# Fewer, longer loads at the head of a vision-tower kernel: chunks three and four of the embedding together, two late weights in whole rows

## The chip, the cores and the metric

One core of a Trainium2 chip runs the whole kernel in one launch. The metric is device time in microseconds (us); the host only lays the arrays out beforehand. Before the change three runs took 125.57, 114.17 and 115.2 us, a median of 115.2 us. The execution that the profiler recorded took 115.0 us, of which 112.8 us are the span of the trace.

## The reference

The input is 16 images of 3x96x96. One transformer block runs on them, with a norm after each half:

- **Embedding.** Each image becomes 36 patches of 768 numbers, times a 768x192 weight, plus a bias.
- **Windowed attention.** 12 heads of 64, a window of 65 tokens, an output weight of 768x192, a residual and a layer norm.
- **Mixture of three attention experts.** Each has 64 channels and a causal mask; the first has a convolution over its queries, the second global keys, the third a position bias (used for at most 64 tokens). A gate picks two of the three. A 192x192 projection, a residual and a layer norm end it.

```python
h = _L0_tok_ref(x, L0_tok_Wp, L0_tok_bp)
h = _layernorm(h + _L0_attn_ref(h, L0_attn_w_qkv, L0_attn_w_out, L0_attn_b_out), axis=-1)
h = _layernorm(h + _L0_ffn_ref(h, ...), axis=-1)
```

## The kernel before, in words

**Tiling.** The 16 images are two groups (g = 0, 1) of eight, 288 tokens each. The 768 patch features are six chunks (k = 0 to 5) of 128, one on each partition row. So `x_f[128, 2, 6, 288]` holds the input and `tw_f[128, 6, 256]` the embedding weight; the weight is 192 wide, and the host repeats its last 64 columns to make 256.

**Split numbers.** TensorE works on a high and a low part of each float32. ScalarE (ACT) makes the high part by a copy, then VectorE (DVE) or GpSimd (POOL) the low part by a subtraction. For embedding chunk n this is step `xs n` on both: ACT writes `tw_hi` (L462) and `x_hi` (L464), DVE `tw_lo` (L648) and `x_lo` (L651). `xs 0` to `xs 5` are the six chunks of group 0 and `xs 6` to `xs 11` those of group 1, whose weights are there already. Step `em n` on TensorE (L884) multiplies chunk n: two halves of the output by three products of high and low parts, six matmuls, each 288 columns wide. Ahead of them TensorE runs 20 warm-up matmuls (L868) and three that clear banks (L871, L873).

**Order.** Three tables, `PE_ORDER`, `ACT_ORDER` and `DVE_ORDER`, set by hand what each engine does after what; an engine that waits holds all that is behind it. They begin:

```python
em 0, em 1, em 2, em 3, em 4, em 5, em 6, em 7, qk 0, em 8, qk 1, em 9, s 0, s 1, v 0 0, qk 2, em 10   # PE
xs 0, xs 1, xs 2, xs 3, xs 4, xs 5, wq 0, xs 6, xs 7, xs 8, wq 1, hh 0, xs 9, cq 0, wv 0, xs 10, wq 2   # ACT
```

`qk` projects queries and keys, `wq` splits their weights, `hh` reads the embedded tokens out, `cq` copies queries and keys, `wv` splits the value weight (L472, then DVE L657 and L659), and `v 0 0` is the first matmul that needs it (L920).

**Loads.** The sync engine (SP) issues nearly every load, one after the other (L367 to L385); ACT issues the first two pieces of the embedding weight. The pieces of group 0's chunks are `X_PIECES`, and `SP_TOK` says which pieces of the weight SP issues. Each piece has a semaphore of its own, so the split of a chunk begins when its piece has landed. After them come biases, query and key weights for the first head pair, group 1's input in two pieces (`X_LATER`, chunks 0 to 2 first: L373) and further weights; the last large ones are `wo_f` (the attention's output weight, L381) and `ffn_f` (the experts' weights, L382), and behind these three small ones, `posb` among them, which DVE reads for `posmask` (L680). The output weight is laid out by the host as six rows of 256 numbers on a partition, the experts' as two rows of 1088; the kernel loads the first 192 and the first 1024 of each row. ACT splits them at L476 (`wo 0`) and L480 (`wf 0`), POOL at L444, L409 and L411.

Of the kernel before, what the change touches and what calls it, by code (L numbers as in the profile page):

```python
# [34 lines left out]
F32 = mybir.dt.float32  # L35
F32R = mybir.dt.float32r
BF16 = mybir.dt.bfloat16
ALU = mybir.AluOpType
ACT = mybir.ActivationFunctionType
# [5 lines left out]
DIM, NCH = 192, 2  # L45
DUP = 256
PATCH, PK = 768, 6
PAIRS, HD = 6, 64
# [14 lines left out]
F_PROJ = F_VAL + DIM  # L63
F_END = F_PROJ + DIM

X_PIECES = [slice(0, 1), slice(1, 2), slice(2, 3), slice(3, 4), slice(4, 6)]
X_LATER = [slice(0, 3), slice(3, 6)]
QK_PIECES = [slice(0, 1), slice(1, 2), slice(2, 4), slice(4, 6)]
WARM_UP = 20
ACT_TOK, SP_TOK = (0, 1), (2, 3, 4)  # L70
TILE_IMAGES = [(0, 3), (3, 6), (6, 8)]
TILES = len(TILE_IMAGES)
ROWS = 3 * TOK
# [71 lines left out]
def vit_tower(nc, x_t, tok_w, w_qk, w_v, w_out, f_w, f_g2, f_bv, pos_bias, biases, consts, bf_consts, out_t):  # L145
    with ExitStack() as ctx:
        def sb(name, shape, dt=F32):
            return ctx.enter_context(nc.sbuf_tensor(name, shape, dt))

        def sem(name):  # L150
            return ctx.enter_context(nc.semaphore(name))
# [12 lines left out]
        wv_f = sb("wv_f", [128, NCH, PATCH])  # L164
        wv_hi = sb("wv_hi", [128, NCH, PATCH], F32R)
        wv_lo = sb("wv_lo", [128, PATCH], F32R)
        wo_f = sb("wo_f", [128, PAIRS, DIM])
        wo_hi = sb("wo_hi", [128, PAIRS, DIM], F32R)
        wo_lo = sb("wo_lo", [128, PAIRS, DIM], F32R)
        ffn_f = sb("ffn_f", [128, NCH, F_END])  # L170
        ffn_hi = sb("ffn_hi", [128, NCH, F_END], F32R)
        ffn_lo = sb("ffn_lo", [128, F_END], F32R)
        fg2_w = sb("fg2_w", [33, 3])
# [63 lines left out]
        ld_const, ld_wv, ld_wo, ld_ffn, ld_small = (sem(s) for s in ("ld_const", "ld_wv", "ld_wo", "ld_ffn", "ld_small"))  # L237
        ld_x = [[sem(f"ld_x{g}{n}") for n in range(len(pieces))] for g, pieces in enumerate((X_PIECES, X_LATER))]
        ld_tok = [sem(f"ld_tok{n}") for n in range(len(X_PIECES))]
        ld_qk = [sem(f"ld_qk{n}") for n in range(len(QK_PIECES))]  # L240
# [4 lines left out]
        qk_hi, qk_lo, wv_hi_s, wv_lo_s, wo_hi_s, wo_lo_s = (  # L245
            sem(s) for s in ("qk_hi", "qk_lo", "wv_hi_s", "wv_lo_s", "wo_hi_s", "wo_lo_s"))
        posmask_s, image_s, conv_b_s = sem("posmask_s"), sem("image_s"), sem("conv_b_s")
        ffn_hi_s, ffn_lo_s, h1_hi_s, h1_lo_s = (sem(s) for s in ("ffn_hi_s", "ffn_lo_s", "h1_hi_s", "h1_lo_s"))
# [99 lines left out]
        def leaving(z):  # L348

            return slice(tile_cols(LEAVE_TILES[z][0]).start, tile_cols(LEAVE_TILES[z][-1]).stop)  # L350
# [8 lines left out]
        def piece_of(g, k):  # L359
            return [n for n, ks in enumerate((X_PIECES, X_LATER)[g]) if ks.start <= k < ks.stop][0]  # L360

# [3 lines left out]
        @block.sync  # L365
        def _(sp):
            for n, ks in enumerate(X_PIECES):  # L367
                if n in SP_TOK:
                    sp.dma_start(tw_f[:, ks], tok_w[:, ks]).then_inc(ld_tok[n], 16)
                sp.dma_start(x_f[:, 0, ks], x_t[:, 0, ks]).then_inc(ld_x[0][n], 16)  # L370
            sp.dma_start(bias[:], biases).then_inc(ld_bias, 16)
            sp.dma_start(wqk_f[:, QK_PIECES[0]], w_qk[:, QK_PIECES[0]]).then_inc(ld_qk[0], 16)
            sp.dma_start(x_f[:, 1, X_LATER[0]], x_t[:, 1, X_LATER[0]]).then_inc(ld_x[1][0], 16)  # L373
            sp.dma_start(wqk_f[:, QK_PIECES[1]], w_qk[:, QK_PIECES[1]]).then_inc(ld_qk[1], 16)
            sp.dma_start(x_f[:, 1, X_LATER[1]], x_t[:, 1, X_LATER[1]]).then_inc(ld_x[1][1], 16)
            sp.dma_start(bfc[:], bf_consts).then_inc(ld_const, 16)
            sp.dma_start(const[:, 0:C_MEAN], consts[:, 0:C_MEAN]).then_inc(ld_const, 16)
            sp.dma_start(wv_f[:], w_v).then_inc(ld_wv, 16)
            for n in (2, 3):
                sp.dma_start(wqk_f[:, QK_PIECES[n]], w_qk[:, QK_PIECES[n]]).then_inc(ld_qk[n], 16)  # L380
            sp.dma_start(wo_f[:], w_out[:, :, 0:DIM]).then_inc(ld_wo, 16)  # L381
            sp.dma_start(ffn_f[:], f_w[:, :, 0:F_END]).then_inc(ld_ffn, 16)  # L382
            sp.dma_start(fg2_w[:], f_g2).then_inc(ld_small, 16)
            sp.dma_start(bv_all[:], f_bv).then_inc(ld_small, 16)
            sp.dma_start(posb[:], pos_bias).then_inc(ld_small, 16)  # L385
            for g in range(GROUPS):
                for z, done in enumerate((outs_a, outs_d)):
                    part = leaving(z)
                    cols = slice(g * GT + part.start, g * GT + part.stop)
                    sp.wait_ge(done, NCH * g + 1)  # L390
                    sp.dma_start(out_t[0:128, cols], out_s[:, g, 0, part]).then_inc(st_out, 16)
                    if (g, z) != (GROUPS - 1, 1):
                        sp.wait_ge(done, NCH * g + 2)
                        sp.dma_start(out_t[128:DIM, cols], out_s[0:64, g, 1, part]).then_inc(st_out, 16)
            sp.wait_ge(st_out, 32 * GROUPS * len(LEAVE_TILES))

        @block.gpsimd
        def _(pool):
            pool.memset(g1_t[:], 0.0).then_inc(zeroed, 1)
            pool.memset(k_t[:, :, :, TOK:KEYS], 0.0).then_inc(zeroed, 1)  # L400
            pool.memset(edges[:], 0.0).then_inc(zeroed, 1)
            pool.memset(wgt_last[:], 0.0).then_inc(zeroed, 1)
            pool.wait_ge(zeroed, 4)
            pool.memset(g1_t[32:33], 1.0).then_inc(zeroed, 1)
            pool.wait_ge(zeroed, ZEROED)

            def lo_part(lo, hi, raw, done, before):

                nc.gpsimd.tensor_tensor(lo, raw[:, 0], hi[:, 0].bitcast(F32), ALU.subtract).then_inc(done, 1)  # L409
                pool.wait_ge(done, before + 1)  # L410
                nc.gpsimd.tensor_tensor(hi[64:128, 1], raw[64:128, 1], hi[64:128, 1].bitcast(F32),  # L411
                                        ALU.subtract).then_inc(done, 1)
                pool.wait_ge(done, before + 2)

            def pair_lo(p):
                pool.wait_ge(qk_hi, p + 1)
                lo_part(wqk_lo[:, p], wqk_hi[:, p], wqk_f[:, p], qk_lo, 2 * p)

            def residual_rows(g, lo_done, col):
                pool.wait_ge(lo_done, NCH * g + NCH)  # L420
                n = pool_sums[0]
                pool_sums[0] += 1
                for c in range(NCH):
                    nc.gpsimd.tensor_tensor(h_res[:, g, c], hcols(h_hi, g, c).bitcast(F32),  # L424
                                            bias[:, col + c:col + c + 1].broadcast_to([128, GT]), ALU.add).then_inc(biased, 1)
                for c in range(NCH):
                    pool.wait_ge(biased, NCH * n + c + 1)
                    nc.gpsimd.tensor_tensor(h_res[:, g, c], h_res[:, g, c], hcols(h_lo, g, c).bitcast(F32),  # L428
                                            ALU.add).then_inc(h_res_s, 1)

            pool_sums = [0]
            pair_lo(0)
            pool.wait_ge(ld_const, 32)
            nc.gpsimd.tensor_copy(edges[:, 0:EDGE], bfc[:, 128 + TOK - EDGE:128 + TOK]).then_inc(band_s, 1)
            nc.gpsimd.tensor_copy(edges[:, FIRST:FIRST + EDGE], bfc[:, 128:128 + EDGE]).then_inc(band_s, 1)
            pair_lo(1)
            pair_lo(2)
            for p in range(3, PAIRS):
                pair_lo(p)
            pool.wait_ge(ld_bias, 16)  # L440
            for g in range(GROUPS):
                residual_rows(g, h_lo_s, B_OUT)
            pool.wait_ge(wo_hi_s, 1)
            nc.gpsimd.tensor_tensor(wo_lo[:], wo_f[:], wo_hi[:].bitcast(F32), ALU.subtract).then_inc(wo_lo_s, 1)  # L444
            pool.wait_ge(wo_lo_s, 1)
            pool.wait_ge(ffn_hi_s, 1)
            lo_part(ffn_lo[:], ffn_hi[:], ffn_f[:], ffn_lo_s, 0)
            for g in range(GROUPS):
                residual_rows(g, h1_lo_s, B_FFN)

        @block.scalar
        def _(act):
            for n in ACT_TOK:
                act.dma_start(tw_f[:, X_PIECES[n]], tok_w[:, X_PIECES[n]]).then_inc(ld_tok[n], 16)
            act.preload_act_table_set("natural_log_exp_and_others")
# [17 lines left out]

            def out_weights():
                act.wait_ge(ld_wo, 16)
                nc.scalar.activation(wo_hi[:], wo_f[:], ACT.Copy).then_inc(wo_hi_s, 1)  # L476

            def ffn_weights():
                act.wait_ge(ld_ffn, 16)
                nc.scalar.activation(ffn_hi[:], ffn_f[:], ACT.Copy).then_inc(ffn_hi_s, 1)  # L480

            def embedding_hi(g):

# [752 lines left out]
```

## Time and profile before

| what | us |
|---|---|
| median of three runs | 115.2 |
| the profiled execution | 115.0 |
| its span in the trace | 112.8 |
| TensorE matmuls busy in the span | 101.0 (90%) |
| VectorE busy | 78.4 (69%) |
| ScalarE busy | 71.1 (63%) |
| GpSimd busy | 29.8 (26%) |

How to read it: TensorE is busy for nine tenths of the span, and its granted clock is in the top tenth in all 40 slices. The 16 DMA engines are busy from about 2 us to about 21 us and nearly idle afterwards: all of the 6.81 MB that is read comes in then. Rows of the timeline give start, duration, engine, line, what is written and read, and in square brackets how long the engine had idled and what ended that. A DMA's row on SPq is its issue, not its transfer; the view of DMAs has the time from an issue to the landing.

### The profile page before, as it was taken

How to read it: one execution, taken by the hardware profiler on the slowest of the kernel's cores; microseconds unless marked ns; L12 is line 12 of the kernel's file. 1: busy time of each engine (PE TensorE's matmuls, PEld its weight loads, DVE VectorE, ACT ScalarE, POOL GpSimd, SP SyncE). 2: the span in 40 equal slices, each digit the busy share in tenths (PEclk: the TensorE clock that was granted, in tenths of full speed). 3: DMA queues.
4: the chain of work that ended last, by engine and by line, in shares of the span. 5: the costliest groups of instructions: out<-in, count | busy, mean ns of one | idle time of the engine just before them, and what ended most of it. 6: DMA issues, size and time to landing. Idle time of an engine off the chain costs nothing.

```text
span 112.8 us, 3470 instructions
## 1 busy us (share of the span) xinstructions
PE 101.0 (90%) x1349; PEld 90.4 (80%) x1349; DVE 78.4 (69%) x239; ACT 71.1 (63%) x198; POOL 29.8 (26%) x42
## 2 busy tenths in 40 slices
PE   6999799999999999999999999999959868797940
PEld 4698699799898899799988998999958767684910
DVE  0555827983992976508695897987868779988670
ACT  4656949387559974895865659672366456558360
POOL 4002543969941700000393540000004500000000
PEclk9999999999999999999999999999999999999999
DMA  3999999500000000000000000000000000000202
GB/s 75 332 307 349 397 400 381 176 5 0 6 0 9 3 0 6 0 0 6 0 0 0 6 6 0 0 6 0 0 3 6 3 0 0 6 0 0 72 12 79
DMA packets 5179, 7.47 MB, mean 66 GB/s; under 512 B 1324, under 2 KB 3756, under 8 KB 5164
## 3 DMA queue, kind: packets, MB, share of 16 engines
q1 hardware_dynamic: 4796, 6.98, 18.1%
q10 hardware_dynamic: 368, 0.28, 0.8%
q8 instruction: 11, 0.18, 0.6%
q14 instruction: 4, 0.03, 0.1%
HBM read 6.81 MB, written 0.44 MB: 64 GB/s over the span
## 4 chain that ended last, share of the span: by engine, by line
PE 60%; DVE 16%; ACT 7%; DMA 5%; issue 5%; SPq 4%; DVEq 0%; ACTq 0%
PE proj L920 11%; PE outp L1050 7%; PE score L1005 7%; DMA x_f<-x_t 5%; PE proj L905 4%; PE trans L1029 3%; PE outp L884 3%; PE proj L906 3%; PE proj L909 3%; PE proj L912 3%; PE proj L913 3%; SPq L370 2%; PE proj L1067 2%; ACT ln_ln L562 2%; DVE ln_st L733 2%
## 5 line engine op out<-in xcount | busy, mean ns | idle before, releaser
L548 ACT ACTIVATE pt_t<-trans,image_t 108x216 f32<-108x216 f32 (+1 forms) x42 | 14.5, 420 | 1.4 <-PE trans L1029 1.3
L424 POOL TENSOR_TENSOR h_res<-h_hi,bias 128x288 f32<-128x288 f32 x8 | 5.2, 667 | 23.3 <-DVE h_lo L757 23.2
L532 ACT ACTIVATE score<-d_t 128x296 f32<-128x296 f32 (+2 forms) x16 | 6.5, 409 | 6.2 <-DVE d_t L697 6.1
L1005 PE MATMUL score<-k_t,q_t 64*36 64x37 f32 (+1 forms) x416 | 10.3, 196 | 0.0
L1005 PEld LDWEIGHTS score<-k_t,q_t 64*36 64x36 f32 x416 | 9.0, 111 | 1.2 <-issue 0.7
L707 DVE TENSOR_REDUCE sm_t<-score 128x8 f32<-128x288 f32 (+1 forms) x16 | 6.9, 434 | 2.8 <-ACT score L532 2.8
L726 DVE TENSOR_TENSOR x_lo<-outp,x_hi 128x288 fp32r<-128x288 f32 x12 | 5.4, 451 | 4.9 <-ACT x_hi L555 4.8
L694 DVE TENSOR_REDUCE mx_t<-score 128x8 f32<-128x296 f32 (+2 forms) x16 | 7.1, 443 | 2.4 <-PE score L1013 1.3
L920 PE MATMUL proj<-wv_hi,h_hi 128*108 128x384 f32 (+1 forms) x24 | 8.2, 344 | 0.2 <-DVE wv_hi L659 0.2
L508 ACT ACTIVATE q_t<-proj 128x288 f32<-128x288 f32 x12 | 4.9, 412 | 5.2 <-PE proj L913 5.0
L562 ACT ACTIVATE ln_ln<-ln_mv,const 108x1 f32<-108x1 f32 (+1 forms) x12 | 3.5, 293 | 7.4 <-DVE ln_mv L736 7.4
L409 POOL TENSOR_TENSOR wqk_lo<-wqk_f,wqk_hi 128x256 fp32r<-128x256 f32 x6 | 4.5, 752 | 12.9 <-ACT wqk_hi L468 12.8
L905 PE MATMUL proj<-h_hi,wqk_hi 128*128 128x288 f32 x24 | 7.5, 325 | 0.4 <-ACT q_t L508 0.2
L651 DVE TENSOR_TENSOR x_lo<-x_f,x_hi 128x288 fp32r<-128x288 f32 x12 | 6.6, 565 | 1.7 <-ACT x_hi L464 1.6
L697 DVE TENSOR_TENSOR d_t<-score,mx_t 128x296 f32<-128x296 f32 (+2 forms) x16 | 7.2, 450 | 0.5
L718 DVE TENSOR_TENSOR p_t<-score,sm_t 128x288 f32<-128x288 f32 (+1 forms) x16 | 7.1, 443 | 0.6
L409 POOL TENSOR_TENSOR ffn_lo<-ffn_f,ffn_hi 128x1024 fp32r<-128x1024 f32 x1 | 2.4, 2380 | 16.5 <-ACT ffn_hi L480 16.5
L906 PE MATMUL proj<-h_hi,wqk_lo 128*128 128x288 f32 x24 | 6.7, 295 | 0.0
L912 PE MATMUL proj<-h_lo,wqk_hi 128*128 128x288 f32 x24 | 6.7, 294 | 0.0
L913 PE MATMUL proj<-h_lo,wqk_hi 128*128 128x288 f32 x24 | 6.7, 294 | 0.0
L1067 PE MATMUL proj<-wo_hi,x_hi 128*108 128x192 f32 (+1 forms) x24 | 6.4, 268 | 0.0
L428 POOL TENSOR_TENSOR h_res<-h_res,h_lo 128x288 f32<-128x288 f32 x8 | 6.2, 798 | 0.0
(192 smaller groups left out, 337.0 us busy)
## 6 DMA issues: line engine op xcount, KB each, us to landing
wqk_f<-w_qk SPq DMA_DIRECT2D x2, 512.0 KB, 8.0
ffn_f<-f_w SPq DMA_DIRECT2D x1, 1024.0 KB, 12.4
x_f<-x_t SPq DMA_DIRECT2D x2, 432.0 KB, 6.0
wv_f<-w_v SPq DMA_DIRECT2D x1, 768.0 KB, 7.2
x_f<-x_t SPq DMA_DIRECT2D x4, 144.0 KB, 3.1
wo_f<-w_out SPq DMA_DIRECT2D x1, 576.0 KB, 9.4
wqk_f<-w_qk SPq DMA_DIRECT2D x2, 256.0 KB, 5.1
x_f<-x_t SPq DMA_DIRECT2D x1, 288.0 KB, 4.7
```

The lines of the kernel that those rows point to most:

```text
L548: nc.scalar.activation(pt_t[:, n % 2, 0:tiles, :, i], trans[0:ROWS, 0:tiles, :, 0:TOK], ACT.Copy, scale=image_t[:, i:i + 1]).then_inc(spli ...
L694: link(nc.vector.tensor_reduce(mx_t[:, n, 0:slots], s[:, :, 0:width], AX.X, ALU.max))
L697: nc.vector.tensor_tensor(d_t[:, n % 2, 0:slots, 0:width], s[:, :, 0:width], mx_t[:, n, 0:slots].unsqueeze(2).broadcast_to([128, slots, wi ...
L718: nc.vector.tensor_tensor(by_image(p_t[:, n % 2, 0:slots * TOK]), e[:, :, 0:TOK], share.unsqueeze(2).broadcast_to([128, slots, TOK]), ALU. ...
L905: nc.tensor.matmul(b, w_hi[:, 0, c], hcols(h_hi, g, 0), start=True, stop=False)
L906: nc.tensor.matmul(b, w_lo[:, c], hcols(h_hi, g, 0), start=False, stop=False)
L912: nc.tensor.matmul(b, w_hi[:, 0, c], hcols(h_lo, g, 0), start=False, stop=False)
L913: nc.tensor.matmul(b, w_hi[:, 1, c], hcols(h_lo, g, 1), start=False, stop=True).then_inc(projected, 1)
L920: ins = nc.tensor.matmul(out, htile(h, c, g, j), w, start=(n == 0), stop=(n == len(ops) - 1))
L1005: ins = nc.tensor.matmul(s[64 * h:64 * h + TOK, im, 0:width], q, k_t[rows, n % QK_RING, im, 0:width], start=(kind == "attn" and im == 0), ...
L1050: ins = nc.tensor.matmul(outp[n % 2][HD * h:HD * h + HD, tile_cols(j)], val[0:rows, j, d:d + HD], probs, start=True, stop=True)
L1067: nc.tensor.matmul(b[0:rows, 0:DIM], o_hi[:, g, p, cols], wo_hi[:, p, 0:DIM], start=False, stop=False, skip_group_check=True)
```

## The change

The third and the fourth chunk of the embedding (k = 2 and 3) are loaded together, input and weight: `X_PIECES` has four entries and no longer five, and SP issues two weight pieces and no longer three. `wo_f` and `ffn_f` are as wide in SBUF as in DRAM, 256 and 1088 columns, and each is loaded whole: a partition's 6144 bytes and 8704 bytes stand in one run. What reads them takes the first 192 and 1024 columns, as before.

```diff
-X_PIECES = [slice(0, 1), slice(1, 2), slice(2, 3), slice(3, 4), slice(4, 6)]
+X_PIECES = [slice(0, 1), slice(1, 2), slice(2, 4), slice(4, 6)]
-ACT_TOK, SP_TOK = (0, 1), (2, 3, 4)
+ACT_TOK, SP_TOK = (0, 1), (2, 3)
...
-        wo_f = sb("wo_f", [128, PAIRS, DIM])
+        wo_f = sb("wo_f", [128, PAIRS, DUP])
...
-        ffn_f = sb("ffn_f", [128, NCH, F_END])
+        ffn_f = sb("ffn_f", [128, NCH, F_PROJ + DUP])
...
-            sp.dma_start(wo_f[:], w_out[:, :, 0:DIM]).then_inc(ld_wo, 16)
-            sp.dma_start(ffn_f[:], f_w[:, :, 0:F_END]).then_inc(ld_ffn, 16)
+            sp.dma_start(wo_f[:], w_out).then_inc(ld_wo, 16)
+            sp.dma_start(ffn_f[:], f_w).then_inc(ld_ffn, 16)
...
-            nc.gpsimd.tensor_tensor(wo_lo[:], wo_f[:], wo_hi[:].bitcast(F32), ALU.subtract).then_inc(wo_lo_s, 1)
+            nc.gpsimd.tensor_tensor(wo_lo[:], wo_f[:, :, 0:DIM], wo_hi[:].bitcast(F32), ALU.subtract).then_inc(wo_lo_s, 1)
...
-            lo_part(ffn_lo[:], ffn_hi[:], ffn_f[:], ffn_lo_s, 0)
+            lo_part(ffn_lo[:], ffn_hi[:], ffn_f[:, :, 0:F_END], ffn_lo_s, 0)
...
-                nc.scalar.activation(wo_hi[:], wo_f[:], ACT.Copy).then_inc(wo_hi_s, 1)
+                nc.scalar.activation(wo_hi[:], wo_f[:, :, 0:DIM], ACT.Copy).then_inc(wo_hi_s, 1)
...
-                nc.scalar.activation(ffn_hi[:], ffn_f[:], ACT.Copy).then_inc(ffn_hi_s, 1)
+                nc.scalar.activation(ffn_hi[:], ffn_f[:, :, 0:F_END], ACT.Copy).then_inc(ffn_hi_s, 1)
```

On SP, at the head of the queue of loads, the rows are now as follows (- before, + now; `tw_f<-tok_w` is the embedding weight, `x_f<-x_t` the input, and the numbers are partitions and elements on each):

```order
 L370 DMA x_f<-x_t 128x288 x2
-L369 DMA tw_f<-tok_w 128x256
-L370 DMA x_f<-x_t 128x288
-L369 DMA tw_f<-tok_w 128x256
-L370 DMA x_f<-x_t 128x288
+L369 DMA tw_f<-tok_w 128x512
+L370 DMA x_f<-x_t 128x576
 L369 DMA tw_f<-tok_w 128x512
 L370 DMA x_f<-x_t 128x576
```

Four issues of one chunk have become two of two chunks, and everything behind them stands two places nearer to the front. Further down the same queue, at the two late weights:

```order
 L378 DMA wv_f<-w_v 128x1536
 L380 DMA wqk_f<-w_qk 128x1024 x2
-L381 DMA wo_f<-w_out 128x6x192
-L382 DMA ffn_f<-f_w 128x2x1024
+L381 DMA wo_f<-w_out 128x1536
+L382 DMA ffn_f<-f_w 128x2176
 L383 DMA fg_w<-f_g 33x3
 L384 DMA bv_all<-f_bv 128x192
```

Each is one run on a partition and no longer six or two, with more bytes. No instruction of TensorE, VectorE, ScalarE or GpSimd has changed its place.

## Rows read from the trace of the kernel before

**Rows 1.** The page's first line.

```profile
span 112.8 us, 3470 instructions
```

**Rows 2.** Stretches: from:to, length, busy by engine, granted clock, DMA share, GB/s.

```profile
4.00:7.00 3.00, 3.00 (x16) 2.27 (x14) 2.68 (x8) 2.61 (x8) 0.00 (x0) 1.00 0.97 279
7.00:10.00 3.00, 2.88 (x23) 2.67 (x21) 1.49 (x4) 1.57 (x5) 0.00 (x0) 1.00 0.99 354
13.00:16.00 3.00, 3.00 (x25) 3.00 (x24) 1.71 (x4) 1.34 (x5) 1.85 (x4) 1.00 1.00 409
16.00:19.00 3.00, 3.00 (x46) 2.84 (x46) 1.33 (x2) 3.00 (x7) 0.40 (x1) 1.00 1.08 372
21.00:22.00 1.00, 1.00 (x7) 0.84 (x5) 0.97 (x4) 0.49 (x1) 0.92 (x2) 1.00 0.22 63
12.50:20.20 7.70, 7.49 (x113) 7.21 (x113) 4.71 (x8) 5.75 (x13) 3.37 (x6) 1.00 1.04 395
```

**Rows 3.** Timeline of TensorE, matmuls of the embedding.

```profile
6.39 0.44 PE L884 MATMUL score<-x_lo,tw_hi 128*128 128x288 f32 x1
6.63 0.39 PE L884 MATMUL score<-x_hi,tw_lo 128*128 128x288 f32 x1
...
8.71 0.30 PE L884 MATMUL score<-x_hi,tw_lo 128*128 128x288 f32 x1
8.84 0.29 PE L884 MATMUL score<-x_hi,tw_hi 128*128 128x288 f32 x1
...
9.93 0.37 PE L884 MATMUL score<-x_hi,tw_hi 128*128 128x288 f32 x1
...
12.51 0.40 PE L884 MATMUL outp<-x_hi,tw_hi 128*128 128x288 f32 x1 [0.75 <-DVE x_lo L651]
```

**Rows 4.** Timeline of ScalarE: chunks 4 and 5, group 1's chunks, value weight.

```profile
8.13 0.42 ACT L462 ACTIVATE tw_hi<-tw_f 128x256 fp32r<-128x256 f32 x1 [1.23 <-DMA tw_f<-tok_w]
8.84 0.45 ACT L464 ACTIVATE x_hi<-x_f 128x288 fp32r<-128x288 f32 x1 [0.30 <-DMA x_f<-x_t]
11.12 1.11 ACT L464 ACTIVATE x_hi<-x_f 128x288 fp32r<-128x288 f32 x3 [0.67 <-DMA x_f<-x_t]
16.11 1.49 ACT L472 ACTIVATE wv_hi<-wv_f 128x1536 fp32r<-128x1536 f32 x1
```

**Rows 5.** Timeline of VectorE: low part of the input, chunks 2 and 3.

```profile
6.15 0.46 DVE L651 TENSOR_TENSOR x_lo<-x_f,x_hi 128x288 fp32r<-128x288 f32 x1 [0.21 <-ACT x_hi L464]
...
6.93 0.46 DVE L651 TENSOR_TENSOR x_lo<-x_f,x_hi 128x288 fp32r<-128x288 f32 x1
```

**Rows 6.** Timeline of SP's queue, the issues of three loads.

```profile
1.65 0.43 SPq L369 DMA_DIRECT2D tw_f<-tok_w  x1
...
3.54 0.49 SPq L369 DMA_DIRECT2D tw_f<-tok_w  x1
...
5.51 0.43 SPq L373 DMA_DIRECT2D x_f<-x_t  x1
```

**Rows 7.** DMAs, issues at 3.07, 3.54, 4.08, 5.51, 8.04: KB, us to landing.

```profile
x_f<-x_t SPq DMA_DIRECT2D x1, 144.0 KB, 3.4
...
tw_f<-tok_w SPq DMA_DIRECT2D x1, 256.0 KB, 4.6
...
x_f<-x_t SPq DMA_DIRECT2D x1, 288.0 KB, 4.7
...
x_f<-x_t SPq DMA_DIRECT2D x1, 432.0 KB, 5.6
...
wv_f<-w_v SPq DMA_DIRECT2D x1, 768.0 KB, 7.2
```

**Rows 8.** The first readers of late loads, by tile: count, ns min/median/max, first and last start.

```profile
L680 DVE SCALAR_TENSOR_TENSOR posmask<-posb,const x1: 620/620/620, 29.5 to 29.5; 128x36 f32<-128x36 f32 x1
...
L476 ACT ACTIVATE wo_hi<-wo_f x1: 1182/1182/1182, 35.0 to 35.0; 128x1152 fp32r<-128x1152 f32 x1
...
L480 ACT ACTIVATE ffn_hi<-ffn_f x1: 1919/1919/1919, 53.3 to 53.3; 128x2048 fp32r<-128x2048 f32 x1
```

## The prediction, made before the changed kernel was run

> **What bounds the kernel now.** I began with the page: the span is 112.8 us [rows 1], and 115.0 us is the time of that execution, so 2.2 us lie outside the span; I leave them as they are. The median of the runs shown is 115.2, that is 0.2 above the execution I argue from. Two of the three runs are 114.17 and 115.2, the third stands far off, so about 1 us of scatter comes with any time here. All edits are loads, so I read only the stretch in which something is loaded, from the start to 22 us, where the DMA share has dropped to 0.22 [rows 2].
>
> Next I asked who waits for a load. On the timeline of TensorE the embedding's matmuls follow each other at 0.13 us (8.71 to 8.84), and there are two stops. The first matmul of `em 4` starts at 9.93; without a wait it would have come six steps of 0.13 after the start of `em 3` at 8.84, at about 9.63. So 0.3 us are lost there. Then `em 6`, the first of group 1, starts at 12.51, after 0.75 us of idle time that VectorE's `x_lo` ended [rows 3]. Behind both stands ScalarE, which waited 1.23 and 0.30 us for chunks 4 and 5 of weight and input, and 0.67 us for group 1's input, which it could take up at 11.12 [rows 4]. This last wait is the one that matters: from 12.50 to 20.20 TensorE is busy 7.49 of 7.70 us [rows 2], so what `em 6` gains is handed on until `v 0 0`, and from there by the tables' order to the end. The first load on the path that the change can move is therefore group 1's input, issued at 5.51 [rows 6] and landed 5.6 us later, at 11.11 [rows 7].
>
> **The two issues removed.** From 1.65 to 5.51 SP issues eight loads [rows 6], 0.48 us each. Two fewer put all that follows 0.97 us earlier into the queue. The two longer ones may cost 0.49 and not 0.43 each, as the two-chunk issue at 3.54 did [rows 6]; 0.85 is left. An earlier issue is an earlier landing only if the DMA engines had nothing else to do. From 4 to 7 us their share is 0.97, from 7 to 10 it is 0.99 [rows 2]: 0.03 of 3 us were free, 0.1 us. And the wait from issue to landing grows from 3.4 us for 144 KB at 3.07 to 5.6 us for 432 KB at 5.51 [rows 7]: the queue is filling, the engines are behind the issues. By this, issuing earlier is worth 0.1 us at the least and 0.85 at the most.
>
> The Trainium skill says the same as a rule (DMA: Bandwidth & Descriptors, "Issuing engines are not separate DMA queues"): what is issued runs on the same 16 engines anyway, so only sequencer time is saved. By it alone the sum would be 115.0; here the trace agrees as far as the share of 0.97 goes.
>
> **The longer rows.** In these same three microseconds, with the engines busy, only 279 GB/s arrive, against 354 from 7 to 10 and 409 from 13 to 16 [rows 2]. So something besides the amount costs time while single-chunk loads (1,024 and 1,152 bytes a partition) and the pair of chunks 4 and 5 pass. At 354 GB/s the 837 KB of that stretch would take 2.36 us and not 3.0: 0.64 us is the most that merging can give back. The merged loads are 256 + 288 KB = 557,000 bytes, two thirds of 837,000; in proportion, 0.43 us. The low end is nothing: two-chunk loads pass in this stretch already. I take **0.4 us** for issue and rows together, nearer to the rows on rates than to the issue's 0.85, since busy engines speak against the latter; the ends kept are 0 and 0.85.
>
> The Trainium skill would have more of it (Perfetto Trace Analysis, "DMA Optimizations"): transfers under 2 KB carry significant overhead, and batching them can improve throughput dramatically. By that rule the upper end of this sum, 0.85, would be due. The rates of before do rise with the row's length, but no run here separates length from position in the queue.
>
> **The chunk that is delayed.** Chunk 2 has so far landed before chunk 3; now both come when the pair is complete. The pair's input is issued at 1.65 + 0.48 = 2.13 [rows 6], right behind its weight. Before, chunk 3 had landed by 3.07 + 3.4 = 6.47 [rows 7], with exactly the bytes ahead of it that the pair has; the other bound is the latency of a 288 KB load, 2.13 + 4.7 = 6.83 [rows 7]. From landing to the end of the low part it takes 0.45 us on ScalarE [rows 4] and 0.46 on VectorE [rows 5], 0.9 us, and chunk 3's low part ends 0.78 us after chunk 2's (6.93 against 6.15). That gives 6.83 + 0.9 = 7.7 for chunk 2 and 8.5 for chunk 3. TensorE wants them at 8.06 (six steps of 0.13 ahead of 8.84) and at 8.84 [rows 3]. Both are in time with 0.3 us to spare, at worst; price 0. If the cover went, `em 2` would be late, and with it `em 3`, but only beyond another 0.3 + 0.75 us would `em 6` be.
>
> **What passes through.** `em 4` can come 0.3 earlier, `em 6` 0.3 + 0.75, near 1.1 us, before TensorE itself is the limit [rows 3]. So 0.4 passes. The next load on the way is `wv_f`, landed at 8.04 + 7.2 = 15.24 [rows 7], used at 16.11 [rows 4]: 0.87 us of slack, more than 0.85. It passes in full even if `wv_f` does not come earlier. **-0.4 us.**
>
> **Whole rows.** `wo_f` grows from 576 to 768 KB, `ffn_f` from 1024 to 1088. By the rates: from 16 to 19 us, when mostly `wo_f` with its rows of 768 bytes passed, 372 GB/s; with long rows 409 [rows 2]. So 590,000 bytes at 372 are 1.59 us, 786,000 at 409 are 1.92; and `ffn_f` adds 65,500 bytes, 0.16 us. The stream of loads ends 0.5 us later (0.7 if all the 262,000 added bytes came at 372), less the 0.4 of the head, at about 22. Only small loads are behind, and the first reader of anything behind it is `posmask` at 29.5; `wo_f` itself is read at 35.0, `ffn_f` at 53.3 [rows 8]: 7 us of cover, price **0**. ScalarE and GpSimd read as many elements as before, now with gaps between the rows. No row has one read both ways. The bounds: nothing, or at worst what six separate reads cost, 6 x 0.45 us [rows 4] in place of 1.18 [rows 8], 1.5 us on ScalarE at 35 us. The element count doesn't change, so I take 0; the 1.5 is among the side effects below.
>
> **Sum.** 115.0 - 0.4 = **114.6 us**. Against the median of 115.2 it is 0.5% less. About 2%, 2.3 us, is what a measurement of this kernel can tell from no change.
>
> **Rivals.**
> - *Nothing arrives earlier.* The DMA engines are at 0.97 to 0.99 from 4 to 10 us, and the same bytes go through ahead of group 1's input. For it: those shares. Against: the low rate of 279 GB/s. 115.0 us.
> - *The whole issue time comes back.* The slow stretch was a matter of many small loads, and group 1's input lands 0.85 us or more earlier; TensorE's stops at `em 4` and `em 6` nearly vanish, limit 1.1. For it: SP issues 128 to 144 KB each 0.48 us, some 300 GB/s, less than the engines can take later. Against: the growing queue. 115.0 - 1.0 = 114.0 us.
> - *The pair comes too late.* One place, chunk 2 and 3. If the pair takes as long as the 768 KB load, 7.2 us [rows 7], it lands at 9.33, `em 2` starts at 10.2 in place of 8.06, and `em 6` at 10.2 + 4 x 0.79 = 13.4, 0.9 late. A matmul step is 0.13 us there, 288 columns at close to 2.4 GHz; at the start of the embedding, from 6.39 to 6.63, it was 0.24, 288 columns at 1.2 GHz [rows 3], though the granted clock reads 1.00 for the whole stretch [rows 2]. If 2.2 us of idle time brought the slow step back for 24 matmuls, 24 x 0.11 = 2.6 us more: 118.5 us. It decides from a landing later than about 8.2 us. Against it: 6.47 to 6.83 by the rows. The Trainium skill's advice on splitting (Perfetto Trace Analysis, "DMA Optimizations") points this way: smaller pieces let some work start sooner. It gives it for DMA engines that are generally idle, and here they are not.
> - *Side effects.* The read with gaps could cost up to 1.5 us on ScalarE, which is not the busiest engine; a shift of the whole order against the DMAs could win or lose some tenths.
>
> **How the numbers follow.** Forecast, 114.6 (own range 114.2 to 114.9): 0.42. Nothing earlier, 115.0: 0.27. All comes back, 114.0: 0.18. The pair late: 0.04, of which 0.02 over 2%. Side effects and what I haven't seen, between 112 and 118: 0.09, of which 0.05 are faster and 0.02 slower by over 2%. Faster 0.05, same 0.91, slower 0.04. The range takes in the first three cases and the scatter of the runs: 113.4 to 115.8.
>
> **What would show it.** Right: SP's issue of group 1's input near 4.6 and not 5.51; ScalarE takes it up at about 10.7 (before 11.12); `em 6` starts at about 12.1; a rate from 4 to 7 us well over 279; `em 2` and `em 3` without a stop; the large loads done near 22. Wrong: ScalarE at 11.1 as before (first rival), at 10.2 or earlier (second), idle time of TensorE ahead of `em 2` (third). A change of over 1.1 us would mean that it came from a place I haven't looked at, behind 20 us.

## The result, and the profile after

The changed kernel takes 113.78 us (median of 18 runs), the kernel before 114.7 us (18 runs). The ratio is 0.9913, with a 95% interval from 0.9893 to 0.9933: 1.0 us less, between 0.8 and 1.2 us. That is inside the range (113.4 to 115.8) and inside 2%, on the side that was forecast, but two and a half times the 0.4 us of the forecast, and it is the 1.0 us of the second rival (114.0). The prediction held 2% to be the least that a measurement of this kernel can tell from nothing; the interval here is 0.2% to either side. The profiled execution took 113.86 us, its span is 111.7 us, 1.1 us shorter than before [rows 1]. (In every kernel's runs here some can take several us longer than the rest; the ratios leave those out.)

The stretches of the changed kernel, with the columns of [rows 2]; PE is TensorE, and PEld its weight loads:

```profile
4.00:7.00 3.00, 3.00 (x23) 2.60 (x20) 1.95 (x5) 1.90 (x7) 0.00 (x0) 1.00 1.03 343
7.00:10.00 3.00, 2.51 (x19) 2.34 (x18) 2.66 (x7) 2.73 (x8) 0.00 (x0) 1.00 1.00 355
...
16.00:19.00 3.00, 2.95 (x80) 2.66 (x78) 2.37 (x2) 2.86 (x7) 1.37 (x2) 1.00 1.05 432
...
21.00:22.00 1.00, 1.00 (x8) 0.97 (x8) 1.00 (x3) 0.82 (x2) 0.42 (x1) 1.00 0.09 28
12.50:20.20 7.70, 7.49 (x112) 7.19 (x112) 5.07 (x9) 4.97 (x11) 4.33 (x7) 1.00 1.02 411
```

From 4 to 7 us 343 GB/s arrive in place of 279, and the DMA share is 1.03 in place of 0.97: the share of before was no sign that the engines could give no more. [Rows 2] had said so themselves, with shares of 1.04 and 1.08 in other stretches. From 7 to 10 us the rate is that of before (355 and 354). TensorE is as full from 12.5 to 20.2 as before.

SP's queue, issues of the pair's weight, of group 1's input and of the two late weights:

```profile
1.63 0.43 SPq L369 DMA_DIRECT2D tw_f<-tok_w  x1
...
4.50 0.43 SPq L373 DMA_DIRECT2D x_f<-x_t  x1
...
9.36 0.45 SPq L381 DMA_DIRECT2D wo_f<-w_out  x1
9.85 0.44 SPq L382 DMA_DIRECT2D ffn_f<-f_w  x1
```

Group 1's input is issued 1.01 us earlier; a two-chunk issue costs no more than a one-chunk issue. And its landing, with the pair's input beside it (issued at 2.11):

```profile
x_f<-x_t SPq DMA_DIRECT2D x1, 432.0 KB, 5.8
```

```profile
x_f<-x_t SPq DMA_DIRECT2D x1, 288.0 KB, 4.5
```

4.50 + 5.8 = 10.3, where it was 11.1: of 1.01 us of earlier issue 0.2 are lost to a longer wait and 0.8 arrive. ScalarE (ACT) and TensorE at the same places:

```profile
5.51 0.42 ACT L462 ACTIVATE tw_hi<-tw_f 128x256 fp32r<-128x256 f32 x1 [0.41 <-DMA tw_f<-tok_w]
6.61 0.45 ACT L464 ACTIVATE x_hi<-x_f 128x288 fp32r<-128x288 f32 x1 [0.68 <-DMA x_f<-x_t]
...
10.35 1.11 ACT L464 ACTIVATE x_hi<-x_f 128x288 fp32r<-128x288 f32 x3 [0.45 <-DMA x_f<-x_t]
...
15.07 1.49 ACT L472 ACTIVATE wv_hi<-wv_f 128x1536 fp32r<-128x1536 f32 x1
```

```profile
7.69 0.37 PE L884 MATMUL score<-x_hi,tw_hi 128*128 128x288 f32 x1 [0.49 <-DVE x_lo L651]
...
11.34 0.40 PE L884 MATMUL outp<-x_hi,tw_hi 128*128 128x288 f32 x1 [0.23 <-DVE x_lo L651]
```

The pair costs TensorE a new stop of 0.49 us ahead of `em 2`, which is free, since `em 6` waits anyway. ScalarE takes group 1's input 0.77 us earlier (10.35, before 11.12), `em 6` begins 1.17 us earlier (11.34, before 12.51), the value weight is split 1.04 us earlier, and the span is 1.1 us shorter. So between ScalarE and `em 6` another 0.4 us were gained, of which 0.1 is gone again at the value weight. The line of VectorE's low parts shows where; its three instructions of group 1, before and then after:

```profile
L651 DVE TENSOR_TENSOR x_lo<-x_f,x_hi x3: 445/446/855, 11.6 to 12.7; 128x288 fp32r<-128x288 f32 x3
```

```profile
L651 DVE TENSOR_TENSOR x_lo<-x_f,x_hi x3: 447/459/997, 10.8 to 12.1; 128x288 fp32r<-128x288 f32 x3
```

One of the three takes double, in both. At that time GpSimd splits the query and key weights of the first head pair (L411 from 11.41 to 12.13 before, from 10.86 to 11.88 after), so the two meet; whether one slows the other is asked below. In the chain of waits of before it is the first, on which `em 6` hangs:

```profile
11.12 0.45 ACT x_hi L464
11.57 0.02 issue
11.60 0.87 DVE x_lo L651
12.46 0.04 issue
12.51 0.40 PE outp L884
```

After the change the first takes 0.47 us, from 10.82, and `em 6` starts at 11.34; there the long one is a later one.

### The profile page after: what moved, and what is told of

The parts are those of the page before. It is cut to its first block, busy times and chain, and to the rows that moved or that the text cites. A ratio compares the mean times of both kernels' runs of the same rounds, so it can differ in the third digit from the quotient of the medians.

```text
span 111.7 us, 3468 instructions
## 1 busy us (share of the span) xinstructions
PE 100.1 (90%) x1349; PEld 89.8 (80%) x1349; DVE 78.5 (70%) x239; ACT 71.1 (64%) x198; POOL 30.1 (27%) x42
## 3 DMA queue, kind: packets, MB, share of 16 engines
HBM read 7.08 MB, written 0.44 MB: 67 GB/s over the span
## 4 chain that ended last, share of the span: by engine, by line
PE 61%; DVE 16%; ACT 7%; DMA 5%; issue 5%; SPq 3%; DVEq 0%; ACTq 0%
PE proj L920 11%; PE outp L1050 8%; PE score L1005 7%; DMA x_f<-x_t 5%; PE proj L905 4%; PE trans L1029 3%; PE outp L884 3%; PE proj L909 3%; PE proj L906 3%; PE proj L912 3%; PE proj L913 3%; PE proj L1067 2%; ACT ln_ln L562 2%; DVE ln_st L733 2%; PE proj L1072 1%
## 5 line engine op out<-in xcount | busy, mean ns | idle before, releaser
L1005 PE MATMUL score<-k_t,q_t 64*36 64x37 f32 (+1 forms) x416 | 10.3, 196 | 0.0
```

What stands on the lines that cost most here:

```text
L1005: ins = nc.tensor.matmul(s[64 * h:64 * h + TOK, im, 0:width], q, k_t[rows, n % QK_RING, im, 0:width], start=(kind == "attn" and im == 0), ...
```

## The experiments

The theory: SP's issue time held the head of the loads back, and what came free there passed to the end. The rivals: longer rows made the loads faster; the whole rows of the late weights helped; the meeting of VectorE and GpSimd, which fell differently in the two executions, made part of it. All ratios are against the kernel before on the same chip (median 114.6 in the first four runs, 114.8 in the others).

**Pieces alone.**

```diff
-X_PIECES = [slice(0, 1), slice(1, 2), slice(2, 3), slice(3, 4), slice(4, 6)]
+X_PIECES = [slice(0, 1), slice(1, 2), slice(2, 4), slice(4, 6)]
-ACT_TOK, SP_TOK = (0, 1), (2, 3, 4)
+ACT_TOK, SP_TOK = (0, 1), (2, 3)
```

> The kernel before with chunks three and four loaded together, and nothing else; the two late weights are loaded as before. If the gain (0.9 to 1.1 us) comes from the head of the loads, it is all here: 1.0 us less than before, the same as the whole change, group 1's input taken up at about 10.35 us in place of 11.12. If the whole rows of the late weights had a part in it, this run gains clearly less than 0.9 us.

Measured 113.59 us, ratio 0.9923 [0.9894, 0.9952]. The whole gain is here. Its profile shows once more what the DMA share is worth:

```profile
4.00:7.00 3.00, 3.00 (x17) 2.28 (x15) 2.01 (x5) 1.86 (x6) 0.00 (x0) 1.00 0.97 328
```

The share is 0.97, that of before to the digit, and the rate is 328 GB/s and not 279.

**Whole rows alone.** The rest of the change, with the five pieces of before.

> The kernel before with the two late weights in whole rows, and nothing else. If they are hidden, the time is that of before within 0.2 us, although their loads end later; ScalarE's copies of 1152 and 2048 elements take 1.18 and 1.92 us as before. If gaps between rows cost on ScalarE, up to 1.5 us more.

Measured 114.87 us, ratio 1.0019 [0.9993, 1.0046]: nothing, or up to 0.5 us slower. ScalarE's reads with gaps, at L476 and L480:

```profile
L476 ACT ACTIVATE wo_hi<-wo_f x1: 1181/1181/1181, 34.2 to 34.2; 128x1152 fp32r<-128x1152 f32 x1
```

```profile
L480 ACT ACTIVATE ffn_hi<-ffn_f x1: 1918/1918/1918, 52.5 to 52.5; 128x2048 fp32r<-128x2048 f32 x1
```

The gaps cost nothing that can be seen (1181 and 1918 ns, before 1182 and 1919). Since its head is that of before, this run is also a second profile of that head, and it is a warning: ScalarE took group 1's input here at

```profile
10.53 1.11 ACT L464 ACTIVATE x_hi<-x_f 128x288 fp32r<-128x288 f32 x3 [0.18 <-DMA x_f<-x_t]
```

and not at 11.12. Between these two executions this moment moved by 0.6 us.

**Issues without longer rows.** ScalarE's queue issues four weight pieces, the five pieces stay.

```diff
-ACT_TOK, SP_TOK = (0, 1), (2, 3, 4)
+ACT_TOK, SP_TOK = (0, 1, 2, 3), (4,)
```

> The kernel before with its five pieces and their rows of 1,024 and 1,152 bytes, but ScalarE's queue issues four of the weight's pieces in place of two: SP has two issues fewer ahead of group 1's input, and no row is longer. If SP's issue time was what held the loads back, group 1's input is issued near 4.55 and taken up at about 10.3 to 10.5, and the time falls by 0.8 to 1.1 us. If the longer rows made the gain, the engines are no faster here: taken up at 10.9 or later, and at most 0.3 us gained.

Measured 114.17 us, ratio 0.9931 [0.9906, 0.9957], 0.8 us gained. The profile has the issue at 4.50 and

```profile
4.00:7.00 3.00, 3.00 (x23) 2.61 (x20) 1.91 (x6) 2.06 (x6) 0.00 (x0) 1.00 1.05 336
```

```profile
10.22 1.11 ACT L464 ACTIVATE x_hi<-x_f 128x288 fp32r<-128x288 f32 x3 [0.36 <-DMA x_f<-x_t]
```

336 GB/s with the short rows of before: the rows' length is not needed for the higher rate. Two things differ from the kernel before, though: SP has two issues fewer, and two more loads go through a second queue beside SP's. This run alone does not separate them.

**Longer rows, the issues spent again.**

```diff
...
+            for n in range(2):
+                sp.dma_start(unused[:, n], biases).then_inc(ld_unused, 16)
             sp.dma_start(bias[:], biases).then_inc(ld_bias, 16)
```

> Chunks three and four together as in the first run, but SP issues two further tiny loads (the biases, 7.5 KB each, into a tile that nobody reads) ahead of the biases: the long rows stay, and the two issues saved are spent again. If issue time was the cause, the gain is gone: group 1's input is issued near 5.5 and taken up at 10.9 to 11.1, time within 0.3 us of before. If the rows' length was the cause, most of it stays: taken up at about 10.5, 0.6 us or more gained.

Measured 114.24 us, ratio 0.996 [0.9931, 0.999]: 0.5 us gained, between 0.1 and 0.8. In the middle about half the gain is gone and half stays, which neither theory had; the interval also overlaps that of the pieces alone. In the profile (its execution took 119.3 us, so I read only its head) group 1's input is issued at 5.43 and taken up at

```profile
10.62 1.11 ACT L468 ACTIVATE x_hi<-x_f 128x288 fp32r<-128x288 f32 x3 [0.42 <-DMA x_f<-x_t]
```

The run doesn't cleanly give the rows' share: the two extra issues stand behind the embedding's pieces, so chunks 4 and 5 were still issued 1 us earlier than before. That a load which is issued no earlier lands somewhat earlier, because those ahead of it had been, fits the issue theory as well as the rows. From 4 to 7 us 350 GB/s arrive in this profile, as many as in the changed kernel, with group 1's input issued as late as in the whole-rows run (5.43).

**GpSimd moved out of the way, in the kernel before.**

```diff
             pool_sums = [0]
+            pool.wait_ge(x_lo_s, 7)
             pair_lo(0)
```

> The kernel before, but GpSimd starts the split of the first head pair's weights only when VectorE has made the low part of group 1's first chunk, about 12.05 in place of 10.60. If that low part took 0.88 us and not 0.45 because GpSimd ran beside it, it takes 0.45 now, group 1's first matmul starts at about 12.1 in place of 12.51, and the time falls by 0.2 to 0.4 us. If it was long for another reason it stays at 0.88, and the time rises by up to 0.3 us if the queries of pair one then wait for GpSimd.

Measured 114.96 us, ratio 0.9993 [0.9962, 1.0025]: no gain. `em 6` does come sooner after ScalarE's start (11.80 after 10.81, 0.99 us; before 1.39, but 1.07 in the whole-rows run, where nothing was moved), but the next step pays: `qk 0` starts at 13.68, 2.87 us after ScalarE's start, against 2.89 in the whole-rows run (13.42 after 10.53).

**The same in the changed kernel.**

> The changed kernel, but GpSimd starts the split of the first head pair's weights only when VectorE has made the low part of group 1's first chunk. In the changed kernel the two meet one instruction later than in the kernel before, so if the meeting was a term of the gain, little is left to win here: within 0.15 us of the changed kernel. If they still meet where it counts, 0.2 to 0.4 us are gained.

Measured 114.15 us, ratio 0.9947 [0.9917, 0.9978]: if anything 0.4 us worse than the changed kernel, whose interval it overlaps. In neither kernel does moving GpSimd gain anything.

**More on ScalarE's queue.** The changed kernel, and of its weight pieces ScalarE issues three, then all four.

```diff
-ACT_TOK, SP_TOK = (0, 1), (2, 3)
+ACT_TOK, SP_TOK = (0, 1, 2), (3,)
```

The second run has `(0, 1, 2, 3), ()` there.

> The changed kernel, with the weight of chunks three and four issued by ScalarE's queue: SP has one issue fewer ahead of all other loads. If issue time still bounds the head, group 1's input is taken up 0.3 to 0.45 us earlier than 10.35, and the kernel gains 0.2 to 0.5 us on the changed one. If the DMA engines bound it by now, nothing changes within 0.1 us.

> The changed kernel, with all four weight pieces issued by ScalarE's queue: SP issues only the input at the head, two issues fewer. If issue time still bounds, group 1's input is taken up up to 0.8 us earlier, but the stop ahead of the third chunk may take over, since TensorE is the limit at about 1.1 us below the changed kernel's start of group 1: 0.3 to 0.9 us gained on the changed kernel. If the DMA engines bound it, at most 0.1 us. ScalarE's table load moves behind four issues and could cost up to 0.3 us at the first chunk.

Measured 114.75 us, ratio 0.9999 [0.9969, 1.0029], and 114.7 us, ratio 0.9996 [0.9971, 1.002]. Both lose the whole gain, against every case that I had written down. With three pieces on ScalarE's queue the pair's weight is issued at the same time as in the changed kernel (1.66 against 1.63) and lands after 5.9 us in place of 3.9:

```profile
tw_f<-tok_w ACTq DMA_DIRECT2D x1, 256.0 KB, 5.9
```

```profile
7.57 0.42 ACT L462 ACTIVATE tw_hi<-tw_f 128x256 fp32r<-128x256 f32 x1 [2.44 <-DMA tw_f<-tok_w]
```

```profile
8.96 0.37 PE L884 MATMUL score<-x_hi,tw_hi 128*128 128x288 f32 x1 [2.03 <-DVE x_lo L651]
```

A likely reason, not shown by itself, is that SP's later loads now move beside it. TensorE stops for 2.03 us ahead of `em 2`, ScalarE gets to group 1's input only when it is done with the rest, and `em 6` is late by itself. With three pieces the granted clock stays at 1.00 from 7 to 13 us. With four the stop is 2.76 us, and in the profiled execution (117.16 us) the granted clock falls soon after TensorE has gone on at 9.89:

```profile
10.00:13.00 3.00, 3.00 (x15) 3.00 (x16) 2.79 (x8) 3.00 (x9) 1.08 (x2) 0.59 1.06 415
```

0.59 is a mean of 3 us; from 11 to 14 us it is 0.50 to 0.51, the 1.2 GHz level, and from 14 us 1.00 again. This does not explain the lost gain: eight of the twelve runs took 114.4 to 114.9 us at a mean clock of 0.994 or more, and a fall of this size would leave at most 0.985 (an estimate: 1.7 us' worth of clock missing in 115). That is the third rival of the prediction, in a kernel one line away; in the changed kernel itself the stop is 0.49 us and the clock stays at 1.00.

**Biases later; three pieces; both.** From the changed kernel again. The first edit:

```diff
-            sp.dma_start(bias[:], biases).then_inc(ld_bias, 16)
             sp.dma_start(wqk_f[:, QK_PIECES[0]], w_qk[:, QK_PIECES[0]]).then_inc(ld_qk[0], 16)
             sp.dma_start(x_f[:, 1, X_LATER[0]], x_t[:, 1, X_LATER[0]]).then_inc(ld_x[1][0], 16)
             sp.dma_start(wqk_f[:, QK_PIECES[1]], w_qk[:, QK_PIECES[1]]).then_inc(ld_qk[1], 16)
+            sp.dma_start(bias[:], biases).then_inc(ld_bias, 16)
```

The second:

```diff
-X_PIECES = [slice(0, 1), slice(1, 2), slice(2, 4), slice(4, 6)]
+X_PIECES = [slice(0, 1), slice(1, 3), slice(3, 6)]
-ACT_TOK, SP_TOK = (0, 1), (2, 3)
+ACT_TOK, SP_TOK = (0,), (1, 2)
```

> The changed kernel, with the biases issued behind group 1's first input piece and the second pair's weights, where ScalarE still gets them in time (it first reads them near 11.9). All order among the large loads stays, and SP has one issue fewer ahead of group 1's input. If issue time still bounds the head: group 1's input issued near 4.0, taken up 0.2 to 0.4 us earlier, 0.2 to 0.4 us gained on the changed kernel. If the 16 engines bound it by now: within 0.1 us.

> The changed kernel with three pieces: chunk 1 alone, 2 and 3 together, 4 to 6 together; ScalarE's queue issues the first weight piece only. All of the larger pieces' weights are in SP's queue, so no queue overtakes another, and one issue fewer stands ahead of group 1's input (three fewer than before the change). If issue time bounds: 0.2 to 0.4 us gained on the changed kernel. If larger pieces now hold TensorE back ahead of the second or fourth chunk by more than the 0.4 us it has spare at group 1: as the changed kernel or up to 0.5 us slower.

> Both of the two before: biases later and three pieces, two issues fewer ahead of group 1's input than in the changed kernel. Issue time: 0.4 to 0.7 us gained, if TensorE, which is at most 0.4 us behind its own limit at group 1 in the changed kernel, lets it: so 0.4. DMA engines: within 0.1 us.

> The changed kernel as it is, beside the three others on the same chip, so that they can be compared with it and not only with the kernel before: 0.9 to 1.1 us less than before. A second profile of it shows how far the time at which group 1's input is taken up (10.35 in the first) varies by itself; in the three profiles with the head of before it was 11.12, 10.53 and 10.81.

| kernel | us | ratio to before, interval |
|---|---|---|
| changed kernel again | 113.99 | 0.9926 [0.9893, 0.9959] |
| biases later | 113.84 | 0.9916 [0.9885, 0.9948] |
| three pieces | 114.76 | 0.9987 [0.9958, 1.0016] |
| both | 114.49 | 0.9978 [0.9954, 1.0001] |

Biases later can't be told from the changed kernel. Its profile is the shortest seen (span 111.1; group 1's input is issued at 4.03 and taken up at 9.51, without a wait), but that execution was also the shortest of its nine, and the medians differ by 0.15 us. The intervals are too wide to decide between the 0.2 to 0.4 us that issue time would give and the 0.1 of a bound in the engines. Three pieces lose most of the gain, with the biases later ("both") as well, where I had expected 0.4 us more; and not because group 1's input is late:

```profile
7.05 0.37 PE L884 MATMUL score<-x_hi,tw_hi 128*128 128x288 f32 x1 [0.60 <-DVE x_lo L651]
9.34 0.38 PE L884 MATMUL score<-x_hi,tw_hi 128*128 128x288 f32 x1 [0.46 <-DVE x_lo L651]
```

```profile
10.41 1.10 ACT L464 ACTIVATE x_hi<-x_f 128x288 fp32r<-128x288 f32 x3
```

TensorE stops ahead of `em 1` and of `em 3`, the first chunks of the second and third piece, and ScalarE comes to group 1's input at 10.41 without a wait for it: the input is there, but the chunks before it came in lumps that are too large. No version here beats the changed kernel by more than the noise.

## Why the prediction was right, and where it was too small

**The place: right.** The gain arises at group 1's input and passes through. Over all profiles but the two above 117 us, from the start of `qk 0` to the end it takes 98.5 to 99.0 us; in the two of before and after, 98.6 (14.2 to 112.8, and 13.2 to 111.7). `wv_f` was no obstacle.

**The size: the step that failed is the 0.4 us "for issue and rows together".** I read a DMA share of 0.97 and a growing wait as engines with no room, and gave the issue 0.1 us at the least, taking a value near the rates. The share doesn't carry that: at 0.97 the run with the pieces alone moves 328 GB/s. With the same row lengths and two of SP's issues on ScalarE's queue the rate rose from 279 to 336 GB/s and 0.8 us were gained. In the two profiles 0.8 of 1.0 us of earlier issue arrive. The upper end that I kept, 0.85, was the better value, and the case that came is the second rival's, to which I had given 0.18: ScalarE's start, 10.35 in the first profile and 10.25 in the mean below, is near its sign (10.2 or earlier) and not the forecast's 10.7. The time fell into the range because the range took that rival in. Of the 0.8 us between 114.6 and 113.78, 0.3 are the starting point (115.0 in one execution, 114.7 as the median of 18). The issue's spacing pointed to the larger value: 128 to 144 KB each 0.48 us are some 300 GB/s, less than the 409 that the engines gave later, and I had that number only in a rival.

**How sure that is.** One profile of each overstates it. The head of before was recorded in three profiles, with ScalarE's start at 11.12, 10.53 and 10.81 (mean 10.8); the changed head in four, 10.35, 9.97 (pieces alone), 10.41 (GpSimd moved) and 10.28 (again), mean 10.25. That is 0.57 us of the 0.8 to 1.2 that the ratio gives. From there to `qk 0` it took 3.1, 2.9 and 2.9 us before and 2.8 to 2.9 after, another 0.1. The 0.4 us at the low part of `x_lo` in the first two profiles is thus mostly an accident of one execution, and with GpSimd moved nothing was gained. About 0.7 us are accounted for by these means; the rest, up to the 0.9 to 1.0 of the ratios, is within their scatter.

**Rows or issues: not fully settled.** Issues alone give 0.8 us (0.5 to 1.1), the spent issues leave 0.5 (0.1 to 0.8). Shown is that longer rows aren't needed. That they do nothing isn't shown. In the issues-alone run a second queue carried more of the loads, so issue time and the second queue aren't separated there; in the pieces-alone run the issues saved and the rows aren't. Nor were the engines simply short of issued work: in the kernel before, SP and ScalarE had issued 1.38 MB by 4.03 us and 1.68 MB by 5 us, and 0.65 and 0.96 MB had arrived by then (sums of the rates of each us). Why the loads of that head run at 275 to 280 GB/s from 4 to 7 us, in all three of its profiles, stays open, and with it how fewer issues raise the rate.

**The delayed chunk: right in kind.** I expected landings between 6.47 and 6.83; 2.11 + 4.5 is 6.6. I said no stop ahead of `em 2`; there is one of 0.49 us, because the embedding itself began earlier (`em 0` at 5.37, before 6.01, behind the warm-up) and not because the pair came late; in the run with the pieces alone, where `em 0` started as late as before, there is no stop. It cost nothing, for the reason given: `em 6` had time to spare.

**Whole rows: right.** 0 us. From 16 to 19 us the rate is 432 against 372 GB/s (409 was assumed), and so in all profiles: 424 to 435 with whole rows, 365 to 381 without; all loads were done sooner than I had said, the share from 21 to 22 us is 0.09, although 4% more is read (7.08 MB, before 6.81). The bound of 1.5 us for reads with gaps came to nothing.

## What to carry to other kernels

Where a queue issues small loads one after the other, compare bytes per issue interval with the rate that the engines reach later. Here it was lower (300 against 409 GB/s), and two issues fewer, 0.97 us of SP's time, gave 0.8 us with the short rows and 1.0 with the long ones although the DMA share stood at 0.97; do not read a share near 1 as full engines. Merge only chunks whose consumers have slack: one more step of merging, or the next pieces on a second queue, gave most or all of the gain back through a stop at the chunk that came late. And before a difference of tenths between two profiles is explained, look at a second profile of the same head.

## What I had not expected of the hardware

- A load issued from ScalarE's queue beside a filled SP queue took 5.9 us for 256 KB (6.8 with four pieces there), where the same load at the same time in SP's queue took 3.9.
- The experts' weights as two rows of 4,096 bytes a partition held SP's queue for 1.30 us, as one run of 8,704 bytes for 0.44 us (0.44 to 0.47 in all nine profiles with whole rows, 1.30 to 1.69 in the five without). The rows of the issue, before and then after:

```profile
10.92 1.30 SPq L382 DMA_DIRECT2D ffn_f<-f_w  x1
```

```profile
L382 SPq DMA_DIRECT2D ffn_f<-f_w x1: 455/455/455, 10.4 to 10.4; - x1
```

The second is from the run with whole rows alone, where everything ahead but the output weight is as before. It gained nothing here, since only loads that are read much later stand behind it; ahead of an urgent load it would count.
